# Transformer layer with block-mean attention and 16 experts: block means from turned x on VectorE, another order of projections and spreads, reciprocals and rotations through PSUM, late experts loaded two a pair

## The chip, the cores and the metric

The kernel runs on one core of a Trainium2 chip. The metric is the device time of one execution in microseconds, here the median of three runs.

## The reference

x is 2 batches of 1024 rows of 256. The layer normalises x, adds an attention with 16 heads over 4 key heads, and adds an expert layer in which each row goes to 4 of 16 experts (hidden size 224). The shortened form is:

```python
xn = _layernorm(x, axis=-1)
q_sem, k_sem = split(xn @ Wq_sem, H, DS), split(xn @ Wk_sem, HKV, DS)
q_geo, k_geo = _rope(split(xn @ Wq_geo, H, DG)), _rope(split(xn @ Wk_geo, HKV, DG))
v = split(xn @ Wv, HKV, DV)
# keys and values older than the last 128 positions: one mean per 64 of them
k_sem2, k_geo2, v2 = pool(k_sem), pool(k_geo), pool(v)
scores = (q_sem k_sem2 + q_geo k_geo2) / sqrt(32) * exp(logit_scale)     # masked by position
attn = softmax(scores) @ v2 @ Wo
w, idx = top_k(softmax(xn @ router_w.T + expert_bias), 4)
ffn = sum over the 4 experts of w * (silu(xn @ gate) * (xn @ up)) @ down
return x + attn + ffn
```

Only the last 128 positions keep keys of their own. Before them stand 14 block means of 64 positions, so each query sees at most 142 keys.

## The kernel before

The five engines run programs written out by hand, which wait for one another by semaphores. Rows are handled in 16 tiles of 128: 8 positions ("t") times 2 batches ("u" or "b"). The order of the work is the order in which each engine's function is written. It has five stages.

1. **Head** (0 to about 40 us). Rows are normalised, turned by TensorE into `xT`, projected to keys (k_geo) and router logits. VectorE picks the four experts of each row and computes the place (`slot`) of each row in a list that is sorted by expert. From there on GpSimd scatters the rows into DRAM (`xn_by_expert`, L716): 16 groups of 4 indirect DMAs, and after each group it waits until all 4 have landed. It has nothing else in its queue until then except, in the last four groups, the four halves of the low parts of experts 4 and 5 (`split_low`, L689 to L696). After the groups stand the low parts of experts 6 to 12, and only behind these the scatters of the expert loop (L743).
2. **Keys** (about 40 to 67 us). Block means of x are made by TensorE (`mean_rows`), copied to SBUF, turned back by TensorE and copied again to `x_keys`. Block means of k_geo are made by `block_means`. `rep_keys` makes the keys of each key head; `rope_q` on VectorE (L1148 to L1160) rotates the queries of the last position's tile: bank times cosine to q1, bank times sine to q2, q1 + q2. `bound_tasks` plans which tile of sorted rows belongs to which expert.
3. **Last tile's units** (about 67 to 126 us). The last 128 positions of each batch see all 142 keys. Eight units (2 batches by 4 key heads) go through `l_score` (TensorE), `l_largest` (VectorE), `l_exp` (ScalarE), `l_probabilities` (VectorE), `l_turn` (TensorE), `l_keep` (ScalarE), `l_value` (TensorE) and `l_values` (VectorE). Two score buffers alternate. Beside unit n each engine does a piece of other work (`beside`): folding value means with Wo, tables of the tasks, high and low parts of the first experts' weights.
4. **Pairs** (about 126 to 204 us). The other seven positions see only block means. For each pair of tiles t = 0 to 6: `rope` (VectorE) and `q_turn`, `q_project`, `score`, `p_turn`, `attend` (TensorE), `shifted`, `row_sum`, `probabilities`, `attended` (VectorE), exponentials and copies on ScalarE. `probabilities` (L1297 to L1305) takes one reciprocal of 32 sums into `srec` in SBUF and multiplies `pr` by it in place. SyncE loads the weights of experts 4 to 13 in this stage (`load_late`); ScalarE makes their high parts as `SPLITS` says, in the pair whose number is the place in the list.
5. **Expert loop** (204 to 414 us). 79 tasks of 128 sorted rows. SyncE loads the rows (`xg`) once all scatters of stage 1 have landed (L643 and the wait for `xs_in`), TensorE turns them and multiplies them with high and low parts (L1366 is the line of all its matmuls), ScalarE copies the result to one of four buffers `y` (L939), GpSimd adds it into the output (L743). From the fifth task on the copy waits for the scatter four tasks back, since the buffers are four. Experts 14 and 15 are loaded once the loop has begun.

In the names of the profile `bank` is a PSUM bank, `q` are q1 and q2, `pr` the probabilities of the pairs, `lex` those of the last tile's units, `wgu` and `wdn` expert weights with `_hi` and `_lo` parts, `x_keys` the block means of x and the last 128 positions, `xr` the residual rows.

## Time and profile before

| | us |
|---|---|
| median of 3 runs | 414.18 (413.63 to 416.24) |
| the profiled execution's own time | 415.77 |
| its span, from the first to the last instruction | 414.0 |
| TensorE busy, VectorE, ScalarE, GpSimd | 357.0, 251.3, 184.1, 232.3 |

Busy time of TensorE is modelled from pipelined matmuls. GpSimd's includes its DMA instructions. PEclk in the views is the clock that TensorE was granted, as a share of 2.4 GHz.

### The profile page before, as it was taken

What the parts mean: (1) busy time and instruction counts of PE and PEld (TensorE: products, weight loads), DVE (VectorE), ACT (ScalarE), POOL (GpSimd) and SP (SyncE); (2) the same over time, 40 slices, a digit from 0 to 9 for tenths busy, and PEclk for the clock granted to TensorE, in tenths of its full rate; (3) what the DMA queues carried; (4) which work ended last, traced back from release to release, by engine and by line L of the source; (5) the groups of instructions that cost most, each with busy time, mean ns of one, the idle gap of its engine ahead of it and who ended that gap; (6) DMA issues with size and microseconds to landing.
All of it is one profiled execution on the core that took longest, in us unless ns stands there. A gap on an engine that the chain in (4) does not pass through costs nothing.

```text
span 414.0 us, 8237 instructions
## 1 busy us (share of the span) xinstructions
PE 357.0 (86%) x2103; PEld 287.1 (69%) x2104; DVE 251.3 (61%) x762; ACT 184.1 (44%) x533; POOL 232.3 (56%) x207
## 2 busy tenths in 40 slices
PE   0598997865998999829899799999999999999991
PEld 0493465432665677615688699999999999999881
DVE  3889665446546868897644755555555555555540
ACT  1541345534601445301556545555555555555550
POOL 0600564646653555794076546666666666666664
PEclk9999999889899989986989989999999999999996
DMA  8991121222427996330239647677667767677544
GB/s 255 357 312 37 65 87 55 84 89 81 123 78 226 294 269 194 104 117 13 61 104 247 119 70 114 112 105 112 112 105 110 117 105 110 112 109 110 79 52 51
DMA packets 50095, 52.33 MB, mean 126 GB/s; under 512 B 5633, under 2 KB 47121, under 8 KB 50073
## 3 DMA queue, kind: packets, MB, share of 16 engines
q0 software_dynamic: 14640, 19.34, 28.4%
q1 hardware_dynamic: 35432, 32.73, 28.0%
q8 instruction: 10, 0.16, 0.2%
q14 instruction: 13, 0.10, 0.1%
HBM read 30.14 MB, written 21.91 MB: 126 GB/s over the span
## 4 chain that ended last, share of the span: by engine, by line
PE 72%; DVE 12%; issue 5%; DMA 4%; SPq 3%; ACT 3%; POOLq 1%; DVEq 0%
PE bank L1366 60%; PE bank L1722 4%; PE bank L1746 4%; DMA xg<-xn_by_expert 2%; DMA x_all<-in_L_attn_x 1%; PE bank L1493 1%; PE bank L1526 1%; DVE wgu_lo L1200 1%; DVE lex L1190 1%; ACT x_all L765 1%; DMA out_rows<-y,idx 1%; SPq L636 1%; DVE q L1160 1%; DVE q L1153 1%; DVE q L1156 1%
## 5 line engine op out<-in xcount | busy, mean ns | idle before, releaser
L743 POOL DMA_INDIRECT out_rows<-y,idx x79 | 124.1, 1571 | 71.2 <-ACT y L939 42.1
L716 POOL DMA_INDIRECT xn_by_expert<-x_all,slot_i x64 | 65.2, 1019 | 56.1 <-DMA xn_by_expert<-x_all,slot_i 32.3
L1346 DVE SCALAR_TENSOR_TENSOR act<-bank,xg,sg 128x224 f32<-128x224 f32 x79 | 35.6, 450 | 55.8 <-ACT sg L926 55.8
L1366 PE MATMUL bank<-wgu_hi,xh 128*128 x158 | 65.3, 413 | 2.6 <-DVE wdn_lo L1201 2.5
L1366 PE MATMUL bank<-wgu_lo,xh 128*128 x158 | 58.9, 373 | 0.0
L1366 PE MATMUL bank<-wgu_hi,xl 128*128 x158 | 58.3, 369 | 0.0
L926 ACT ACTIVATE sg<-bank 128x224 f32<-128x224 f32 x79 | 28.3, 359 | 62.5 <-PE bank L1366 62.5
L1366 PE MATMUL bank<-wdn_hi,ah 112*128 x158 | 51.6, 327 | 0.6 <-issue 0.5
L1338 DVE TENSOR_TENSOR xl<-bank,xh 128x256 fp32r<-128x256 f32 x79 | 33.5, 424 | 29.1 <-ACT xh L917 29.1
L1366 PE MATMUL bank<-wdn_hi,al 112*128 x158 | 44.7, 283 | 0.0
L1366 PE MATMUL bank<-wdn_lo,ah 112*128 x158 | 44.5, 281 | 0.0
L939 ACT COPY y<-bank 128x256 f32<-128x256 f32 x79 | 29.5, 374 | 27.7 <-PE bank L1366 27.7
L1366 PEld LDWEIGHTS bank<-wgu_hi,xh 128*128 128x128 f32 x158 | 30.0, 190 | 5.1 <-issue 3.1
L1354 DVE TENSOR_TENSOR al<-bank,ah 112x256 fp32r<-112x256 f32 x79 | 32.7, 414 | 0.5 <-ACT ah L930 0.5
L1722 PE MATMUL bank<-const_k,xg 128*128 128x128 f32 x158 | 30.7, 275 | 2.5 <-DMA xg<-xn_by_expert 2.5
L1366 PE MATMUL bank<-wqg,xT 128*128 128x512 f32 x64 | 32.5, 635 | 0.0
L1366 PEld LDWEIGHTS bank<-wgu_hi,xl 128*128 128x128 f32 x158 | 30.1, 190 | 2.7
L917 ACT CAST xh<-bank 128x256 fp32r<-128x256 f32 x79 | 29.9, 378 | 3.4 <-PE bank L1722 3.0
L1366 PEld LDWEIGHTS bank<-wgu_lo,xh 128*128 128x128 f32 x158 | 30.3, 192 | 1.2
L1366 PEld LDWEIGHTS bank<-wdn_hi,ah 112*128 112x128 f32 x158 | 30.1, 191 | 1.2 <-issue 1.1
L1746 PE MATMUL bank<-const_k,act 128*112 128x128 f32 x158 | 30.3, 273 | 0.0
L1366 PEld LDWEIGHTS bank<-wdn_lo,ah 112*128 112x128 f32 x158 | 30.3, 192 | 0.0
(240 smaller groups left out, 679.4 us busy)
## 6 DMA issues: line engine op xcount, KB each, us to landing
xg<-xn_by_expert SPq DMA_DIRECT2D x79, 129.0 KB, 2.5
wgu<-in_L_ffn_gate_proj SPq DMA_DIRECT2D x16, 224.0 KB, 6.0
wgu<-in_L_ffn_up_proj SPq DMA_DIRECT2D x16, 224.0 KB, 6.7
wdn<-in_L_ffn_down_proj SPq DMA_DIRECT2D x16, 224.0 KB, 7.4
x_all<-in_L_attn_x SPq DMA_DIRECT2D x8, 256.0 KB, 4.6
xr<-in_L_attn_x SPq DMA_DIRECT2D x14, 128.0 KB, 3.3
out_rows<-xr SPq DMA_DIRECT2D x14, 128.0 KB, 1.7
out_rows<-y,idx POOLq DMA_INDIRECT x79, 3.8
```

What stands on the lines that cost most here:

```text
L636: tile = sp.value_load(td_i[0:1, ds(j, 1)], min_val=0, max_val=N * K // P - 1)
L716: gp.indirect_dma_start(xs_d, bass.IndirectOffsetOnAxis(slot_i[:, z, r:r + 1], 0), x_all[:, z, :], None).then_inc(xs_in[p], DMA)
L743: gp.indirect_dma_start(out_rows, bass.IndirectOffsetOnAxis(idx[r % RING][:, 0:1], 0), ysb[r % 4][:, :], None, compute_op=ALU.add).then_in ...
L917: nc.scalar.copy(xh[t.par][:, :, :], bank[t.par][:, 0:D].rearrange("p (c n) -> p c n", c=DC)).then_inc(xh_ready, 1)
L926: nc.scalar.activation(sg[t.par][:, :], bank[2 + t.par][:, 0:I], ACT.Silu).then_inc(sg_ready, 1)
L939: nc.scalar.copy(ysb[t.place][:, :], bank[6 + t.par][:, 0:D]).then_inc(y_ready, 1)
L1338: nc.vector.tensor_tensor(xl[t.par][:, :, :], bank[t.par][:, 0:D].rearrange("p (c n) -> p c n", c=DC), xh[t.par][:, :, :].bitcast(F32), AL ...
L1346: nc.vector.scalar_tensor_tensor(av[t.par][:, :], bank[2 + t.par][:, I:2 * I], xg[t.slot][:, D + 1:D + 2], sg[t.par][:, :], ALU.mult, ALU. ...
L1354: nc.vector.tensor_tensor(al[t.par][:, :, :], bank[4 + t.par][0:IH, 0:2 * P].rearrange("p (c n) -> p c n", c=2), ah[t.par][:, :, :].bitcas ...
L1366: return nc.tensor.matmul(o, lhsT, rhs, start=start, stop=stop)
L1722: last = nc.tensor.transpose(bank[t.par][:, c * P:(c + 1) * P], xg[t.slot][:, c * P:(c + 1) * P], ident)
L1746: last = nc.tensor.transpose(bank[4 + t.par][0:IH, c * P:(c + 1) * P], av[t.par][:, c * IH:(c + 1) * IH], ident)
```

## The change

- **Block means of x.** `mean_rows`, the copy to `x_mean` and the four turns back go. VectorE reduces each `xT[t]` over blocks of 64 columns instead, 14 reductions of 128x256, and scales the 56 means once. ScalarE copies the last position's columns into `x_keys` right after the turns.
- **Order of the keys stage.** TensorE projects the last tile's queries before the rest of the key means, and uses other banks. VectorE rotates the last tile's queries before `weights(1)`; `bound_tasks` moves from ahead of the units to beside unit 1, the spread of its table from unit 1 to 2. The first score no longer waits for `vloc_kept` and `starts_read`. The last two folds stand beside units 3 and 4.
- **Order within the units.** VectorE computes the probabilities of unit n + 1 ahead of the maximum of unit n + 2 and of the side work of unit n. Its low parts of experts 0 and 1 stand beside units 4 and 5.
- **PSUM.** `rope_q` writes bank times cosine back into the bank and adds q2 to that. `srec` becomes two reciprocals of 16 sums each in the bank of the turned probabilities.
- **Late experts.** SyncE loads 4 and 5 ahead of the pairs as before, but 6 to 11 two at a time after the stores of pairs 0, 1 and 2. `SPLITS` moves their high parts one or two pairs later.

```diff
-        RANK_BANK, MEAN_BANK, BLOCK_BANK = 6, 7, 6
-        REP_BANKS = (2, 3, 4, 5, 2, 3, 4, 5)
-        L_Q, L_QS, VLOC_BANK = (7, 0), (1, 2), 6
+        RANK_BANK, BLOCK_BANK = 6, 7
+        REP_BANKS = (4, 5, 0, 1, 4, 5, 7, 0)
+        L_Q, L_QS, VLOC_BANK = (2, 3), (0, 1), 6
         V_BANK, ASEM_BANKS = 4, (0, 4)
-        SPREAD_AT, ASEM_AT = 1, 5
-        FOLDS = {1: (0,), 2: (1,), 3: (2, 3)}
-        FOLD_BANKS = (4, 4, 4, 0)
-        STARTS_BANK = 1
+        SPREAD_AT, ASEM_AT = 2, 5
+        FOLDS = {1: (0,), 2: (1,), 3: (2,), 4: (3,)}
+        FOLD_BANKS = (4, 4, 4, 4)
+        STARTS_BANK = 0
         HIGH_AT = {0: 0, 1: 1, 5: 2}
-        SPLITS = ((), (4, 5), (6, 7), (8, 9), (10,), (), ())
+        SPLITS = ((), (4, 5), (), (6, 7), (8, 9), (10,), ())
         HEAD = (11, 12)
         SENT = 11
         BETWEEN = (4, 5)
...
+            load_residual(1)
             load_late(0)
-            load_residual(1)
-            load_late(1)
-            load_late(2)
-            load_late(3)
             load_residual(REMOTE - 1)
...
             for i in range(REMOTE - 3):
                 store_sum(i)
                 load_residual(i + 2)
-                if i == 1:
+                if i < 3:
+                    load_late(i + 1)
+                else:
                     load_behind(4, 2)
+            store_sum(REMOTE - 3)
             load_behind(5, 4)
-            store_sum(REMOTE - 3)
...
+            act.wait_ge(xT_ready, TB)
+            for b in range(NB):
+                last = nc.scalar.copy(x_keys[:, :, b, NBLK:NKEY], xT[REMOTE][:, b, :, :])
+            last.then_inc(means_kept, 1)
...
-            act.wait_ge(means_done, 1)
-            nc.scalar.copy(x_mean[:, :, :].rearrange("p b n -> p (b n)"), bank[MEAN_BANK][0:NBLK, :]).then_inc(means_rows, 1)
-            act.wait_ge(means_turned, 1)
-            for b in range(NB):
-                at = b * DC * NBLK
-                nc.scalar.copy(x_keys[:, :, b, 0:NBLK], bank[MEAN_BANK][:, at:at + DC * NBLK].rearrange("p (c n) -> p c n", c=DC))
-                last = nc.scalar.copy(x_keys[:, :, b, NBLK:NKEY], xT[REMOTE][:, b, :, :])
-            last.then_inc(means_kept, 1)
...
-            act.wait_ge(hscale_ready, 1)
-            for n in range(HKV):
-                keep_rep(n)
             act.wait_ge(pooled, REMOTE)
             nc.scalar.copy(k_mean[:, :, :].rearrange("p b n -> p (b n)"), bank[BLOCK_BANK][0:NBLK, 0:NB * KD]).then_inc(blocks_rows, 1)
+            for u in range(NB):
+                act.wait_ge(l_qs, u + 1)
+                nc.scalar.copy(qsT[u][:, :, :], bank[L_QS[u]][:, :].rearrange("p (g n) -> p g n", g=HKV)).then_inc(l_qsT, 1)
             act.wait_ge(keys_turned, 1)
             for b in range(NB):
                 nc.scalar.copy(kgeo_t[:, b, 0:NBLK], bank[BLOCK_BANK][:, b * NBLK:(b + 1) * NBLK])
                 last = nc.scalar.copy(kgeo_t[:, b, NBLK:NKEY], bank[BLOCK_BANK][:, (1 + b) * P:(2 + b) * P])
             last.then_inc(keys_kept, 1)
-            act.wait_ge(l_qs, 1)
-            nc.scalar.copy(qsT[0][:, :, :], bank[L_QS[0]][:, :].rearrange("p (g n) -> p g n", g=HKV)).then_inc(l_qsT, 1)
-            for n in range(HKV, 2 * HKV):
+            act.wait_ge(hscale_ready, 1)
+            for n in range(2):
+                keep_rep(n)
+            for u in range(NB):
+                act.wait_ge(l_qt, u + 1)
+                nc.scalar.copy(qrT[u][:, :, :], bank[L_Q[u]][:, :].rearrange("p (g n) -> p g n", g=HKV)).then_inc(l_qT, 1)
+            for n in range(2, 2 * HKV):
...
+
+            def rope_q(raw_bank, u, t, done):
+
+                raw = raw_bank[:, :].rearrange("p (g h d) -> p g h d", g=H, h=2)
+                t2 = q2[:, :].rearrange("p (g h d) -> p g h d", g=H, h=2)
+                co = cos[:, ds(t * RH, RH)].rearrange("p (o d) -> p o d", o=1).to_broadcast([P, 2 * H, RH])
+                for half in range(2):
+                    sn = sin[:, ds(t * DS + half * RH, RH)].rearrange("p (o d) -> p o d", o=1).to_broadcast([P, H, RH])
+                    last = nc.vector.tensor_tensor(t2[:, :, half, :], raw[:, :, 1 - half, :], sn, ALU.mult)
+                link(last)
+                by_half = raw_bank[:, :].rearrange("p (g d) -> p g d", d=RH)
+                link(nc.vector.tensor_tensor(by_half, by_half, co, ALU.mult))
+                nc.vector.tensor_tensor(q1[u][:, :], raw_bank[:, :], q2[:, :], ALU.add).then_inc(done, 1)
+
+            for t in range(REMOTE):
+                dve.wait_ge(xT_ready, t + 1)
+                for b in range(NB):
+                    last = nc.vector.tensor_reduce(x_keys[:, :, b, 2 * t:2 * t + 2], xT[t][:, b, :, :].rearrange("p c (k n) -> p c k n", n=MB), axis=AX.X, op=ALU.add)
+            link(last)
+            nc.vector.tensor_scalar(x_keys[:, :, :, 0:NBLK], x_keys[:, :, :, 0:NBLK], 1.0 / MB, None, ALU.mult).then_inc(means_kept, 1)
+            for u in range(NB):
+                dve.wait_ge(l_q, u + 1)
+                if u:
+                    dve.wait_ge(l_rope, u)
+                rope_q(bank[L_Q[u]], u, REMOTE, l_rope)
...
-                nc.vector.tensor_tensor(q1[u][:, :].rearrange("p (g d) -> p g d", d=RH), raw_bank[:, :].rearrange("p (g d) -> p g d", d=RH), co, ALU.mult)
-                for half in range(2):
-                    sn = sin[:, ds(t * DS + half * RH, RH)].rearrange("p (o d) -> p o d", o=1).to_broadcast([P, H, RH])
-                    last = nc.vector.tensor_tensor(t2[:, :, half, :], raw[:, :, 1 - half, :], sn, ALU.mult)
-                return last
-
-            def rope_sum(u, done):
-                nc.vector.tensor_tensor(q1[u][:, :], q1[u][:, :], q2[:, :], ALU.add).then_inc(done, 1)
...
-                link(rope_q(bank[L_Q[u]], u, REMOTE))
-                rope_sum(u, l_rope)
-            bound_tasks()
...
+                elif n == SPREAD_AT - 1:
+                    bound_tasks()
                 elif n == SPREAD_AT + 1:
                     keep_tables()
-                elif n in (3, 4):
-                    split_low(n - 3)
+                elif n in (4, 5):
+                    split_low(n - 4)
...
             l_largest(0)
             l_largest(1)
+            l_probabilities(0)
             for n in range(UNITS):
-                l_probabilities(n)
+                if n + 1 < UNITS:
+                    l_probabilities(n + 1)
                 if n + 2 < UNITS:
                     l_largest(n + 2)
...
-                link(rope_q(bank[2 + u], u, t.number))
-                rope_sum(u, c_rope[u])
+                rope_q(bank[2 + u], u, t.number, c_rope[u])
...
-                nc.vector.reciprocal(srec[:, :, :], ssum[:, :, :]).then_inc(c_rec, 1)
+                srec = [turned_bank(u, t)[:, 0:H] for u in range(NB)]
+                for u in range(NB):
+                    last = nc.vector.reciprocal(srec[u], ssum[:, u, :])
+                last.then_inc(c_rec, 1)
                 dve.wait_ge(c_rec, t.count(1))
                 for u in range(NB):
-                    nc.vector.tensor_tensor(by_key(pr[u], t), by_key(pr[u], t), over_heads(srec[:, u, :], t), ALU.mult).then_inc(c_p[u], 1)
+                    nc.vector.tensor_tensor(by_key(pr[u], t), by_key(pr[u], t), over_heads(srec[u], t), ALU.mult).then_inc(c_p[u], 1)
...
-            def mean_rows(t):
-
-                return mm(bank[MEAN_BANK][0:NBLK, :], sums_of(t), x_all[:, NB * t:NB * (t + 1), 0:D], t == 0, t == REMOTE - 1)
-
...
-            for t in range(4):
-                mean_rows(t)
+            block_means(0)
+            block_means(1)
             pe.wait_ge(chosen_ready, 1)
...
-            for t in range(4, REMOTE):
-                last = mean_rows(t)
-            last.then_inc(means_done, 1)
-            pe.wait_ge(means_rows, 1)
-            for b in range(NB):
-                for c in range(DC):
-                    at = (b * DC + c) * NBLK
-                    last = nc.tensor.transpose(bank[MEAN_BANK][:, at:at + NBLK], x_mean[:, b, c * P:(c + 1) * P], ident[0:NBLK, 0:NBLK])
-            last.then_inc(means_turned, 1)
+            block_means(2)
+            block_means(3)
...
-            pe.wait_ge(slots_ready, 1)
-            block_means(0)
-            block_means(1)
-            pe.wait_ge(kv_in, 4 * DMA)
-            pe.wait_ge(wrep_ready, DC * (G + 2))
-            pe.wait_ge(means_kept, 1)
-            for n in range(HKV):
-                rep_keys(n)
-                block_means(2 + n)
-            block_means(REMOTE - 1)
+            pe.wait_ge(q_in, 2 * DMA)
+            for u in range(NB):
+                for c in range(DC):
+                    last = mm(bank[L_Q[u]][:, :], xT[REMOTE][:, u, c, :], wqg[:, c, :], c == 0, c == DC - 1)
+                last.then_inc(l_q, 1)
+            for t in range(4, REMOTE):
+                block_means(t)
             pe.wait_ge(rope_done, TB)
+            for u in range(NB):
+                for g in range(HKV):
+                    for c in range(DC):
+                        last = mm(bank[L_QS[u]][:, g * P:(g + 1) * P], wqs[:, c, g * P:(g + 1) * P], xT[REMOTE][:, u, c, :], c == 0, c == DC - 1)
+                last.then_inc(l_qs, 1)
...
+            pe.wait_ge(kv_in, 4 * DMA)
+            pe.wait_ge(wrep_ready, DC * (G + 2))
+            pe.wait_ge(means_kept, 2)
+            for n in range(2):
+                rep_keys(n)
             for u in range(NB):
-                for c in range(DC):
-                    last = mm(bank[L_Q[u]][:, :], xT[REMOTE][:, u, c, :], wqg[:, c, :], c == 0, c == DC - 1)
-                last.then_inc(l_q, 1)
-            l_sem(0)
+                pe.wait_ge(l_rope, u + 1)
+                turn_queries(bank[L_Q[u]], u).then_inc(l_qt, 1)
+            pe.wait_ge(l_qsT, NB)
+            for n in range(2, HKV):
+                rep_keys(n)
...
-            pe.wait_ge(starts_ready, 1)
-            pe.wait_ge(l_qsT, 1)
-            mm(bank[STARTS_BANK][:, 0:NT * E], ones[0:1, :], at_of(left[:, :, :])[0:1, 0:NT * E], True, True).then_inc(starts_spread, 1)
-            pe.wait_ge(rep_kept, HKV + 1)
-            l_sem(1)
...
-                    pe.wait_ge(vloc_kept, 1)
                     pe.wait_ge(masks_ready, 3)
-                    pe.wait_ge(starts_read, 1)
...
                 if n == 0:
                     rep_values()
+                    pe.wait_ge(starts_ready, 1)
+                    mm(bank[STARTS_BANK][:, 0:NT * E], ones[0:1, :], at_of(left[:, :, :])[0:1, 0:NT * E], True, True).then_inc(starts_spread, 1)
...
```

VectorE's order in the units, before (units 1 and 2; `lex` and `lrec` alternate between two buffers, `lneg` is the negated maximum, `oT` the attended values):

```order
L1187 RECIPROCAL lrec_211<-lsum_209 128x4
L1188 TENSOR_TENSOR pr_64<-lex_205,lrec_211 128x4x14
L1190 TENSOR_TENSOR lex_205<-lex_205,lrec_211 128x4x128
L1180 TENSOR_REDUCE lneg_207<-bank 128x2 x2
L1196 COPY oT_213<-bank 128x256
L1187 RECIPROCAL lrec_210<-lsum_208 128x4
L1188 TENSOR_TENSOR pr_64<-lex_204,lrec_210 128x4x14
L1190 TENSOR_TENSOR lex_204<-lex_204,lrec_210 128x4x128
```

And after, from the first unit on:

```order
L1181 RECIPROCAL lrec_208<-lsum_206 128x4
L1182 TENSOR_TENSOR pr_64<-lex_200,lrec_208 128x4x14
L1184 TENSOR_TENSOR lex_200<-lex_200,lrec_208 128x4x128
L1181 RECIPROCAL lrec_209<-lsum_207 128x4
L1182 TENSOR_TENSOR pr_64<-lex_201,lrec_209 128x4x14
L1184 TENSOR_TENSOR lex_201<-lex_201,lrec_209 128x4x128
L1174 TENSOR_REDUCE lneg_204<-bank 128x2 x2
L1159 TENSOR_TENSOR vb<-bank,const_c 128x4x56
```

The probabilities of the second unit now stand ahead of the first side work instead of behind it, and so on through all units.

SyncE's queue in the pairs, after: the load of experts 6 and 7 (`wgu`, `wdn`) behind the store of pair 0 (`out_rows`) and the residual rows of pair 2 (`xr`):

```order
L588 DMA out_rows<-xr_0_72 128x256
L588 DMA out_rows<-xr_0_74 128x256
L583 DMA xr_0_72<-in_L_attn_x 128x256
L583 DMA xr_0_74<-in_L_attn_x 128x256
L400 DMA wgu<-in_L_ffn_gate_proj 128x2x224
L401 DMA wgu<-in_L_ffn_up_proj 128x2x224
L402 DMA wdn<-in_L_ffn_down_proj 112x2x256
L400 DMA wgu<-in_L_ffn_gate_proj 128x2x224
L401 DMA wgu<-in_L_ffn_up_proj 128x2x224
L402 DMA wdn<-in_L_ffn_down_proj 112x2x256
```

Before, all 24 loads of experts 4 to 11 stood ahead of the first of these stores.

## Rows read from the trace of the kernel before

**Rows 1.** Stages: busy time of each engine, granted clock, DMA share, GB/s.

```profile
40.36:62.00 21.64, 21.10 (x92) 12.16 (x89) 14.97 (x47) 8.64 (x23) 12.79 (x16) 1.00 0.20 71
67.34:111.81 44.47, 31.99 (x172) 18.13 (x171) 22.76 (x65) 23.36 (x83) 26.17 (x30) 0.88 0.26 88
111.81:126.20 14.39, 13.79 (x60) 9.73 (x59) 8.02 (x16) 2.75 (x8) 7.71 (x10) 1.00 0.24 84
204.40:224.49 20.09, 19.40 (x112) 17.30 (x112) 10.40 (x33) 11.32 (x33) 12.61 (x8) 0.92 0.63 167
224.49:236.00 11.51, 8.10 (x51) 7.05 (x52) 9.21 (x21) 8.23 (x20) 7.21 (x5) 1.00 0.77 145
236.00:405.20 169.20, 168.62 (x1113) 156.49 (x1114) 91.18 (x275) 88.56 (x276) 107.20 (x70) 0.99 0.66 102
```

**Rows 2.** The same view of pairs 0, 4, 5 and 6.

```profile
126.20:134.60 8.40, 7.06 (x40) 4.93 (x41) 5.43 (x14) 1.40 (x3) 3.80 (x5) 1.00 0.90 265
...
163.60:172.00 8.40, 8.40 (x49) 6.28 (x48) 7.30 (x20) 3.40 (x8) 6.55 (x7) 1.00 0.50 173
172.00:196.00 24.00, 14.02 (x56) 8.49 (x54) 21.94 (x24) 2.85 (x9) 18.26 (x12) 0.79 0.19 56
196.00:204.40 8.40, 7.35 (x48) 5.79 (x47) 5.12 (x14) 3.98 (x10) 0.00 (x0) 1.00 0.16 49
```

**Rows 3.** Chain that ended last, in the units: start, us, engine, tile, line.

```profile
68.19 1.56 ACT lex L836 x8
...
94.19 1.00 DVE wgu_lo L1200
...
96.04 0.70 DVE lex L1190
...
96.78 0.66 PE bank L1526 x4
97.44 1.42 PE bank L1366 x10
...
98.89 0.81 DVE lneg L1180 x2
```

**Rows 4.** Timeline at pair 5: start, us, engine, line, operation, tiles.

```profile
174.08 2.09 POOL L693 TENSOR_TENSOR wgu_lo<-wgu,wgu_hi  x1 [0.74 <-DMA xn_by_expert<-x_all,slot_i]
174.17 0.32 DVE L1291 TENSOR_TENSOR pr<-bank,smax 128x160 f32<-128x160 f32 x1
176.25 11.15 DVE L1305 TENSOR_TENSOR pr<-pr,srec 128x160 f32<-128x160 f32 x2
187.19 2.16 POOL L693 TENSOR_TENSOR wgu_lo<-wgu,wgu_hi  x1
```

**Rows 5.** All rotations' sums, L1160: ns min/median/max.

```profile
L1160 DVE TENSOR_TENSOR q<-q,q x16: 691/692/2494, 56.3 to 193.0; 128x512 f32<-128x512 f32 x16
```

**Rows 6.** Scatter of rows: DMA from issue to landing, 40 to 126 us, then 126 to 175.

```profile
DMA to landing us min/median/max: 2.4/2.6/4.5
...
DMA to landing us min/median/max: 2.4/4.6/8.1
```

**Rows 7.** GpSimd's timeline: first and twelfth group, then the loop's first scatter.

```profile
41.30 1.03 POOL L716 DMA_INDIRECT xn_by_expert<-x_all,slot_i  x1 [0.59 <-POOL x_all L706]
...
125.91 0.97 POOL L716 DMA_INDIRECT xn_by_expert<-x_all,slot_i  x1 [2.66 <-DMA xn_by_expert<-x_all,slot_i]
...
216.25 1.62 POOL L743 DMA_INDIRECT out_rows<-y,idx  x1 [1.10 <-ACT y L939]
```

**Rows 8.** ScalarE's timeline: the copy of the fifth task's result.

```profile
224.49 0.37 ACT L939 COPY y<-bank 128x256 f32<-128x256 f32 x1 [0.30 <-PE bank L1366]
```

**Rows 9.** DMA issues: KB each, us to landing.

```profile
xg<-xn_by_expert SPq DMA_DIRECT2D x79, 129.0 KB, 2.5
...
out_rows<-y,idx POOLq DMA_INDIRECT x79, 3.8
```

**Rows 10.** VectorE's timeline in the head: one reduction of 128x256.

```profile
32.68 0.42 DVE L1041 TENSOR_REDUCE weight_sum<-weight_dense 128x16 f32<-128x256 f32 x1
```

More of the change, by code:

```diff
@@ L178, in build @@
         smax = [wat.take(f"smax{u}", [P, H]) for u in range(NB)]
-        ssum, srec = (wat.take(n, [P, NB, H]) for n in ("ssum", "srec"))
+        ssum = wat.take("ssum", [P, NB, H])
         wl = r_loop[0]
@@ L233, in build @@
         kgeo_t = wa.take("kgeo_t", [P, NB, NKEY])
-        x_mean = wa.take("x_mean", [NBLK, NB, D])
         k_mean = wa.take("k_mean", [NBLK, NB, KD])
@@ L292, in build @@
         wl = Region(l_at, S_SIZE - (l_at - s_at))
+        lex = [wl.take(f"lex{q}", [P, G, NKEY]) for q in range(2)]
         qsT = [wl.take(f"qsT{u}", [P, HKV, P]) for u in range(NB)]
-        lex = [wl.take(f"lex{q}", [P, G, NKEY]) for q in range(2)]
         lneg = [wl.take(f"lneg{q}", [P, G]) for q in range(2)]
@@ L1524, in l_turn @@
                     pe.wait_ge(l_pT, n)
+                else:
+                    pe.wait_ge(vloc_kept, 1)
                 for h in range(G):
```

38 lines of the change are left out of this document (8 added, 30 removed).

## The prediction

> **What bounds the kernel now.** I read the table of stages first. In the expert loop from 236 us TensorE is busy 168.6 of 169.2 us at the full clock [rows 1]: that stage is TensorE's own work and the change leaves it alone, so only its start can move. Before it TensorE is idle 12.5 of 44.5 us in the last tile's units, where its clock falls to 0.88 on average [rows 1]. A pair takes 8.4 us with TensorE busy throughout (pair 4), but pair 5 takes 24.0 with TensorE busy 14.0 [rows 2]. Then I read the chain of waits in the units [rows 3], the timeline at pair 5 [rows 4], and last GpSimd's own chain, which is off the path today: scatters from 41.3 us [rows 7] to 174 [rows 4], then seven pairs of low parts, then the first scatter of the loop at 216.25. Since the change shortens the stages beside it, I ask of each stage what it leaves for this chain.
>
> **Keys stage: last tile's units begin 5 us earlier.** From 40.36, where the first weights are done, VectorE is busy 14.97 us up to 62.00 and otherwise waits [rows 1], mostly for TensorE. The plan of tasks after 62.00 moves behind the first unit. New are 14 reductions of 256 elements. One alone takes 0.42 [rows 10]; back to back I take 0.35, so 4.9, and 0.2 for the scale. Each rotation gets one more link, some 0.1 us. So VectorE's work is 15.0 + 5.1 + 0.2 = 20.3, and with 1 us of gaps between linked instructions it ends at 61.6. TensorE's chain in the new order (block means as the rotations of k arrive, projections, keys) comes to its first score at about 60.7 and ends it near 62.2. The first maximum, which stood just inside the 67.34 boundary, then starts at 62.3: -5.0. The means' old way (copies and turns) cost nothing on the path by itself; its bound from below is 0, from above these 5 us. The two waits that leave the first score (table read, local values) are inside the same figure.
>
> **Units: 11 us less.** Today's chain goes, for one unit: probabilities, turn 0.66, score 1.42, maximum 0.81, copy of values, side work (a low part: 1.0 and more), and only then the next probabilities (the link at 96.04 takes 0.70) [rows 3]. The next unit's exponentials have long been ready. With its probabilities computed first, what ties unit n to n + 2 is probabilities 1.0, turn 0.66, score 1.42, maximum 0.81, exponentials 1.56 [rows 3] and waits, 5.7 us for two units. That is below the engines' own sums, so these decide. I walked the eight units through the three queues with these durations and the side work where it now stands: probabilities end at 65.7, 67.3, 72.0, 77.6, 81.2, 86.3, 90.3 and 94.4, and the projection with Wo that began at 111.81 begins at 95.7. The check on this: TensorE's work in the stage is 32 us at a clock of 0.88 [rows 1], some 29 at full clock, and 95.7 - 62.3 = 33.4. So -16.1 at that place, 5.0 of it from the keys. What follows up to 126.20 has TensorE busy 13.8 of 14.4 [rows 1] and keeps its length: the pairs begin at 110.1. The value means travel through DRAM meanwhile; their fold comes later by one unit, and I count 8 us of slack for them.
>
> **Pairs.** At 176.25 VectorE starts two products `pr` times `srec` that take 11.15 us, while GpSimd runs low parts back to back (174.08 to 187.19 and on) [rows 4]. In the same moments the difference of a bank and `smax`, at 174.17, takes 0.32 at the same width [rows 4], so two such would take 0.64 and the excess is 10.5. The held ones have two SBUF inputs. So has the sum of a rotation: 16 of them, 0.692 in the median, 2.494 at most [rows 5]. After the change both have one input in PSUM. The Trainium skill ("SBUF — State Buffer", "Who interferes with whom") says that a VectorE instruction with two SBUF inputs and a GpSimd instruction that reads SBUF exclude each other, and that the second blocks until the first finishes. That the form with PSUM passes, the trace agrees with. That a hold ends with one GpSimd instruction it contradicts: those take 2.1, so two holds would come to 4.2 at most and the rest of the 10.5 would have another cause and stay; by the rows all of it goes.
> I take pairs 0 and 4 at their 8.4 and 1, 2, 3 at 8.5, so 42.3; pair 5 at 10.3 (8.4 and 1.9 for two chunks of probabilities); pair 6 at 8.4 up to the first turned rows of the loop [rows 2]. By this the loop could start at 110.1 + 42.3 + 10.3 + 8.4 = 171.1. Two small costs: the link and the second reciprocal, 0.1 to 0.2 each time, lie under TensorE, which never waits in pair 4; bound 0 to 3 us. And the late experts. Their load now follows the store of the pair before; 6 DMAs of 224 KB at the 265 GB/s of pair 0 [rows 2] take 5.1 us, and ScalarE asks for them 10 to 11 us after that store. I expect it to wait 1 us in each of pairs 3, 4 and 5: +3, bound 0 to 9. So 174.1, against 204.4.
>
> **What is late next: GpSimd.** The scatters land at 174.05 today: GpSimd waits for the last one and starts low parts at 174.08 [rows 4]. Eleven groups take 125.91 - 41.30 = 84.6, 7.69 each [rows 7]. Undisturbed, 16 would end at 41.3 + 15 x 7.69 + 7.0 = 163.7; beside the loads of experts landing grows from 2.6 to 4.6, 8.1 at most [rows 6]. The change brings the same bytes in smaller portions over more groups. I leave the end at 174.05 (bounds 163.7 and, all seven groups from 110 us at 8.1 us, 163.7 + 7 x 5.5 = 202.2). The loop's rows are loaded behind it, 2.5 from issue to landing [rows 9] and 0.8 for SyncE's and TensorE's steps: first turn at 177.4.
> Then GpSimd does seven experts' low parts ahead of its first scatter. Four took 187.19 - 174.08 = 13.1 [rows 4], so 3.28 each and 23.0 in all: 197.0, and 1.1 as today ahead of the scatter: 198.1 [rows 7]. It lands 3.8 later [rows 9]. Only then may ScalarE write the fifth task's result, at 202.0; by TensorE it would be ready at 177.4 + 20.1 = 197.5. Today that copy is at 224.49 [rows 8]. From there everything follows as before: -22.5. What the wait adds by a lower clock (rows 1 show 0.92 over the loop's first 20 us) I set against what it hides of TensorE's idle 3.4 us between 224.5 and 236 [rows 1]: 0.
>
> **Sum.** Span 414.0 - 22.5 = 391.5. The profiled execution took 415.77, 1.59 above the median of 414.18, so by its own time 393.3 and by the median 391.7. Of 5 + 11 + 13 us gained ahead, 8 go to a chain that was hidden. Without GpSimd's chain the sum would be 204.4 - 174.1 = 30.3, so 384.
>
> **Rivals.**
> A. *The pairs stay the bound, since the units gain little.* For it: three queues that wait on one another rarely keep a hand-made schedule, and TensorE's clock falls when it idles. Against it: the chain's side work is plain in the rows. With no gain in the units the loop starts at 174.1 + 11 = 185.1 and nothing behind it waits: 185.1 + 209.6 = 394.7, by the median 394.9. 0.20.
> B. *Smaller portions disturb the scatters less.* They land at 166: low parts end at 189.0, first scatter lands at 193.9; the loop starts by the pairs at 174.1, its fifth result at 194.2: -30.3, 384. For it: a portion ends before the group's last DMA in about half the cases. 0.20.
> C. *They disturb more groups.* With landing doubled in seven groups, 163.7 + 7 x 2.6 = 181.9, 7.8 later: 399.5. The Trainium skill ("DMA: Bandwidth & Descriptors", the paragraph on arbitration) has each DMA engine take turns between its queues packet by packet, which is this case for as long as a load lasts. The rows (2.6 and 4.6) are near it. 0.12.
> D. *Slower than before.* The same mechanism at its worst: each group waits the full 8.1. The scatters land at 202.2, 28.2 later: 391.7 + 28.2 = 419.9. It decides from a mean landing of 7.3 us in the seven groups on, (196.6 - 163.7) / 7 + 2.6. Against it: today's median under a heavier load is 4.6. 0.03.
> E. *The PSUM operand does not end the hold.* The back-to-back low parts fall behind the pairs now, so only the four inline halves hold the pairs, by up to 1 us each. The loop would start at 178.1, still under GpSimd's bound: 391.7 too. The trace would tell, not the time; it is part of the forecast.
>
> **How the numbers follow.** Forecast 0.43 (387 to 396), A 0.20, B 0.20, C 0.12, D 0.03, and 0.02 that some new wait takes nearly all. The range reaches from below B to above C: 382 to 401. A measurement of this kernel tells about 1% from no change. Faster by more: 0.95. Within: 0.02. Slower: 0.03.
>
> **What would show it.** Right: the first maximum near 62, no unit longer than 6 us, the pairs' start near 110; both L1305's and L1160's successors without any instance over 1 us; scatters landed near 174; low parts of experts 6 to 12 without a gap of 17 us among them, the loop's first scatter near 198 and ScalarE's fifth copy waiting for it. Wrong: pair 5 still above 15 us; ScalarE waiting for expert loads over 3 us in a pair; scatters landed after 182 or before 168; the loop from its fifth task on slower than 2.35 us a task.

## The result and the profile after

Four executions of the changed kernel took 394.55 us in the median (390.10 to 399.95), four of the kernel before beside them 415.21. The ratio is 0.947, with an interval of 0.938 to 0.956; ratios leave out executions more than 1.5% above the fastest of their kernel, here the one of 399.95 us. The profiled execution of the changed kernel took 395.17 us with a span of 393.4; the forecast was 391.7 us and a span of 391.5. A second measurement gave 395.13 us and 0.950 (0.944 to 0.957).

The stages of the kernel after, cut at the same places as [rows 1] (busy time of each engine, granted clock, DMA share, GB/s):

```profile
60.97:96.94 35.97, 32.36 (x174) 19.00 (x172) 24.92 (x78) 22.75 (x83) 20.90 (x22) 0.86 0.25 82
96.94:111.36 14.42, 13.79 (x61) 9.75 (x59) 8.15 (x16) 2.76 (x8) 9.08 (x10) 1.00 0.29 103
178.72:203.34 24.62, 23.17 (x127) 20.50 (x128) 9.96 (x30) 11.62 (x34) 23.85 (x16) 0.86 0.58 149
203.34:214.90 11.56, 7.10 (x37) 6.09 (x35) 8.48 (x19) 8.29 (x20) 9.68 (x6) 0.85 0.78 114
214.90:384.60 169.70, 168.85 (x1113) 156.62 (x1114) 91.58 (x277) 88.55 (x276) 107.53 (x70) 0.99 0.65 102
```

The units last 36.0 us instead of 44.5, what follows them 14.4 as before, and the long loop 169.7 instead of 169.2: it has only moved. The third line is the loop's beginning up to the fifth result; there GpSimd is busy 23.85 of 24.62 us, where it was busy 12.61 of 20.09.

The seven pairs in the same view:

```profile
111.36:121.66 10.30, 8.85 (x41) 5.64 (x41) 5.66 (x14) 1.40 (x3) 4.09 (x5) 0.83 0.73 223
121.66:132.14 10.48, 9.90 (x55) 6.62 (x55) 8.35 (x26) 4.82 (x11) 6.04 (x7) 1.00 0.33 102
132.14:140.50 8.36, 8.36 (x50) 6.02 (x48) 6.11 (x17) 1.78 (x5) 4.20 (x6) 1.00 0.67 205
140.50:148.78 8.28, 8.28 (x50) 6.19 (x49) 6.93 (x20) 4.68 (x10) 5.72 (x6) 1.00 0.77 241
148.78:157.22 8.44, 8.44 (x49) 6.30 (x48) 7.51 (x22) 4.30 (x10) 3.76 (x5) 1.00 0.81 257
157.22:168.21 10.99, 10.61 (x55) 7.09 (x53) 9.07 (x25) 4.36 (x12) 7.59 (x8) 1.00 0.83 252
168.21:175.54 7.33, 7.33 (x47) 5.75 (x46) 4.15 (x12) 3.58 (x9) 3.75 (x4) 1.00 0.77 243
```

Pair 5, the sixth line, takes 11.0 us; it took 24.0 [rows 2]. No instruction with the new operand is long. The products with the reciprocals and the sums of the rotations (ns min/median/max), against 11.15 us for two products [rows 4] and 2.494 us for the longest sum [rows 5]:

```profile
L1305 DVE TENSOR_TENSOR pr<-pr,bank x14: 180/284/389, 124.6 to 177.2; 128x32 f32<-128x32 f32 x2, 128x64 f32<-128x64 f32 x2, 128x96 f32<-128x96 f32 x2, 128x128 f32<-128x128 f32 x2
L1084 DVE TENSOR_TENSOR q<-bank,q x16: 691/691/692, 49.4 to 165.3; 128x512 f32<-128x512 f32 x16
```

What ends last now. GpSimd's timeline: its first and last low part behind the scatters, and the loop's first scatter:

```profile
175.91 2.07 POOL L691 TENSOR_TENSOR wgu_lo<-wgu,wgu_hi  x1 [3.33 <-DMA xn_by_expert<-x_all,slot_i]
177.95 1.25 POOL L694 TENSOR_TENSOR wdn_lo<-wdn,wdn_hi  x1
...
195.68 2.12 POOL L691 TENSOR_TENSOR wgu_lo<-wgu,wgu_hi  x1
197.76 1.28 POOL L694 TENSOR_TENSOR wdn_lo<-wdn,wdn_hi  x1
199.20 1.62 POOL L741 DMA_INDIRECT out_rows<-y,idx  x1 [0.16 <-issue]
```

and ScalarE's copies of the fourth and fifth results:

```profile
198.93 0.38 ACT L930 COPY y<-bank 128x256 f32<-128x256 f32 x1 [0.31 <-PE bank L1366]
203.34 0.37 ACT L930 COPY y<-bank 128x256 f32<-128x256 f32 x1 [2.33 <-DMA out_rows<-y,idx]
```

The fourth copy was released by TensorE, the fifth by the first scatter's landing. At 2.38 us a task it would have stood at 201.3. So the chain that was hidden before holds the fifth result by 2.0 us. It also sets the loop's beginning: TensorE is idle 3.2 us ahead of 178.72, until the first rows have come in behind the scatters. The chain that ended last in this trace names it, with 14% for the DMA of the scatters of rows and 13% for their issue, where the page of before had TensorE with 72% and none of these scatters.

### The profile page after: what moved, and what is told of

The parts are those of the page before. It is cut to its first block, busy times and chain, and to the rows that moved or that the text cites. A ratio compares the mean times of both kernels' runs of the same rounds, so it can differ in the third digit from the quotient of the medians.

```text
span 393.4 us, 8217 instructions
## 1 busy us (share of the span) xinstructions
PE 350.6 (89%) x2085; PEld 287.6 (73%) x2086; DVE 242.4 (62%) x784; ACT 182.6 (46%) x530; POOL 232.0 (59%) x207
## 4 chain that ended last, share of the span: by engine, by line
PE 48%; DMA 18%; POOL 14%; issue 9%; DVE 6%; ACT 2%; POOLq 1%; SPq 1%; DVEq 0%; ACTq 0%
PE bank L1366 39%; DMA xn_by_expert<-x_all,slot_i 14%; POOL xn_by_expert L714 13%; PE bank L1728 4%; PE bank L1704 4%; DMA out_rows<-y,idx 2%; DMA x_all<-in_L_attn_x 1%; ACT x_all L763 1%; POOL wgu_lo L691 1%; DVE stats L954 1%; PE bank L1378 1%; DVE logit_left L1024 1%; DMA xg<-xn_by_expert 1%; POOLq L103 0%; ACT wgu_hi L815 0%
## 5 line engine op out<-in xcount | busy, mean ns | idle before, releaser
L714 POOL DMA_INDIRECT xn_by_expert<-x_all,slot_i x64 | 66.2, 1034 | 55.6 <-DMA xn_by_expert<-x_all,slot_i 33.7
```

The lines of the kernel that those rows point to most:

```text
L714: gp.indirect_dma_start(xs_d, bass.IndirectOffsetOnAxis(slot_i[:, z, r:r + 1], 0), x_all[:, z, :], None).then_inc(xs_in[p], DMA)
```

## The experiments

Ratios are to the kernel before, measured beside each kernel. Beside the first four runs (units' order alone, PSUM operands alone, SBUF again, low parts left out) the kernel before took 407.5 to 416.0 us, elsewhere 408.6 to 417.6 with most above 413; their ratios therefore may read up to 1% high, and I compare these four by their times. The times of before go with TensorE's clock: of its 35 executions in this section the 5 with a mean granted clock of 0.96 or more took 409.7 us on average, the 16 below 0.95 took 415.0. A size from these four runs is therefore uncertain by 3 to 4 us, and what they show rests on their traces.

**One part alone, and one part undone.** Before, with the units' order alone:

```diff
+            l_probabilities(0)
             for n in range(UNITS):
-                l_probabilities(n)
+                if n + 1 < UNITS:
+                    l_probabilities(n + 1)
```

> The kernel before, with one edit: each unit's probabilities are computed one unit ahead, as in the changed kernel. Rotations and reciprocals keep their SBUF operands, the late experts load as before. Theory 1 (the hold by GpSimd's back-to-back low parts catches whichever pair's products fall into it): the units end 11 us earlier, pairs start near 115; GpSimd begins its low parts at 174 as before, and now pair 6's products fall into them instead of pair 5's and are held some 10 us; the loop starts 11 us earlier, span near 403, time near 404. Theory 2 (the hold is a matter of pair 5 alone, and once the pairs are early enough it is gone): loop starts 21 us earlier, then GpSimd's chain sets the end: span near 392, time near 393. Theory 3 (the units gain little): pairs start after 122, time above 410.

Measured: 399.97 us, ratio 0.976 (0.967 to 0.985), against a median of 412.5 for before: 12.5 less, by the ratio only 2.4% or some 10. The profiled execution took 408.4, 8 above the rest, with a mean granted clock of 0.945 where the rest had 0.961 to 0.966, so its rows show where time goes and the median shows how much. VectorE's timeline:

```profile
165.02 2.44 DVE L1307 TENSOR_TENSOR pr<-pr,srec 128x160 f32<-128x160 f32 x2
174.91 12.11 DVE L1307 TENSOR_TENSOR pr<-pr,srec 128x192 f32<-128x192 f32 x2
```

Before, the long hold was on the products with 160 columns, which stand beside TensorE's pair 5. Now these take 2.44 us, and the long hold is on the next ones, with 192 columns beside pair 6, since these are what GpSimd's low parts (from 174.87 on) now meet: theory 1, for the place. For the size the median is 4 us below what theory 1 gave; whether the hold is shorter in the other executions no trace shows. Theory 3 falls: the pairs start at 118.9.

Before, with the PSUM operands alone:

```diff
-                nc.vector.tensor_tensor(q1[u][:, :], q1[u][:, :], q2[:, :], ALU.add).then_inc(done, 1)
+                nc.vector.tensor_tensor(q1[u][:, :], raw_bank[:, :], q2[:, :], ALU.add).then_inc(done, 1)
...
-                nc.vector.reciprocal(srec[:, :, :], ssum[:, :, :]).then_inc(c_rec, 1)
+                srec = [turned_bank(u, t)[:, 0:H] for u in range(NB)]
```

> The kernel before, with one edit: the sum of each rotation and the product with the reciprocals take one operand from PSUM. Theory 1 (an operand in PSUM passes GpSimd): no instruction of the two groups above 1 us, pair 5 takes 10 to 13 us instead of 24, the loop starts near 192 and TensorE, not GpSimd, sets the fifth result: span near 402, time near 403. Theory 2 (the port is held for either form): products of 10 us again, time 415 as before.

Measured: 403.3 us, ratio 0.986 (0.975 to 0.997): 9.2 less than the median of before, by the ratio only 1.4% or some 6. All its products:

```profile
L1305 DVE TENSOR_TENSOR pr<-pr,bank x14: 181/284/389, 139.7 to 191.7; 128x32 f32<-128x32 f32 x2, 128x64 f32<-128x64 f32 x2, 128x96 f32<-128x96 f32 x2, 128x128 f32<-128x128 f32 x2
```

Theory 1: pair 5 takes 10.4 us (172.3 to 182.7), with GpSimd's low parts running from 173.5 to 189.9 beside its products.

The changed kernel with the two SBUF forms again (the diff above, turned round):

> The changed kernel with the two SBUF forms of before put back (rotation sum, product with the reciprocals). Theory 1: GpSimd's back-to-back low parts begin at 175.9 and the last pair's products, which end at 177.5, fall into them: held some 8 to 10 us, so the loop's first gate products and with them the fifth result come 5 to 8 us later: time 399 to 403. Theory 2 (the pairs now finish ahead of the low parts, so the form no longer matters): time as the changed kernel, near 394.5, with at most two held instructions of 2 us.

Measured: 400.45 us, ratio 0.980 (0.968 to 0.992), 5.3 to 5.9 us above the changed kernel, and 4.9 in the spans. The last pair's products, and TensorE's turn that waits for them:

```profile
180.16 8.52 DVE L1301 TENSOR_TENSOR pr<-pr,srec 128x224 f32<-128x224 f32 x2
```

```profile
187.36 0.69 PE L1603 MATMUL bank<-const_k,pr 128*128 128x128 f32 x2 [6.04 <-DVE pr L1301]
```

Theory 1. So the operand matters in the changed kernel too, in its last pair, which the prediction had thought to be ahead of the low parts.

The changed kernel with the units' old order (the first diff, turned round):

> The changed kernel with one edit undone: a unit's probabilities are computed only after the side work of the unit before. Theory 1 (the order of the units is worth 11 us, and it reaches the end once the pairs are the bound): pairs start near 122, the loop near 189, the fifth result comes from TensorE near 212 and no longer waits for GpSimd: 7 to 9 us longer than the changed kernel. Theory 2 (scatters and GpSimd's low parts hide most of it): 0 to 3 us longer.

Measured: 404.88 us, ratio 0.975 (0.968 to 0.982), 9.8 us above the changed kernel on the same chip. Pairs start at 127.7, and the fifth result is copied at 214.75 without a wait for a scatter. Theory 1, and a little more than its 7 to 9. The clock has a part in that size: the units took 53.0 us here at 0.74, where before, with the same order of probabilities, they took 44.5 at 0.88.

The changed kernel with the late loads where they were:

```diff
-            load_residual(1)
             load_late(0)
+            load_residual(1)
+            load_late(1)
+            load_late(2)
+            load_late(3)
...
-        SPLITS = ((), (4, 5), (), (6, 7), (8, 9), (10,), ())
+        SPLITS = ((), (4, 5), (6, 7), (8, 9), (10,), (), ())
```

> The changed kernel with one edit undone: experts 4 to 11 are again loaded in one go ahead of the pairs, 12 in pair 1, 13 behind pair 5, and their high parts stand where they stood before. Theory 1 (where the loads stand matters little; the smaller portions cost ScalarE its 12 to 15 us of waits for experts, of which at most 4 reach TensorE, and in return the burst of 5.4 MB against the scatters is gone): ScalarE's waits for expert loads under 5 us in sum, scatters landed between 172 and 180, time within 3 us of the changed kernel's 394.9. Theory 2 (the smaller portions disturb the scatters more, as rival C says): scatters landed before 172, time 4 us shorter or more. Theory 3 (the burst disturbs them more): scatters landed after 181, time 4 us longer or more.

Measured: 392.95 us, ratio 0.953 (0.945 to 0.960): no difference that can be told from the changed kernel's 0.947 and 0.950. Scatters landed at 173.1 and ScalarE waited for no expert, against 10.4 us in the changed kernel (15.4 in its second trace). Theory 1. In this trace the loop began at 176.1, 2.6 us sooner than in the changed kernel's first one, and GpSimd's low parts 2.8 us sooner. The fifth copy came 2.7 us sooner, at the end of a longer wait for the first scatter:

```profile
200.66 0.37 ACT L931 COPY y<-bank 128x256 f32<-128x256 f32 x1 [3.63 <-DMA out_rows<-y,idx]
```

**Both of the first two parts, and nothing else.**

> The kernel before with both edits together: probabilities one unit ahead, and the PSUM operands. What is still missing of the change is the new keys stage (which in the changed kernel starts the units 6 us earlier), the new places of the side work and the late loads two a pair. Pairs start near 119 (as with the first edit alone) and the loop some 64 us later (as with the second alone), near 183; GpSimd's scatters land near 174 and its fifth-result bound stands near 202, TensorE's near 204. Theory 1 (once the pairs are early enough GpSimd's chain sets the end, so that the missing 6 to 9 us are mostly hidden): 393 to 397, at most 2 us above the changed kernel. Theory 2 (the pairs' start decides to the end): 400 to 403.

Measured: 394.8 us, ratio 0.954 (0.949 to 0.959), beside 0.947 and 0.950 for the whole change. For the time theory 1: two edits give the whole gain within what can be measured. Alone they took 12.5 and 9.2 us off by the medians (2.4 and 1.4% by the ratios), together 19.4 (4.6%), so the times leave open whether anything is missing to the sum. The trace shows a part that is hidden: its fifth copy waits 4.6 us for GpSimd:

```profile
196.46 0.37 ACT L939 COPY y<-bank 128x256 f32<-128x256 f32 x1 [0.31 <-PE bank L1368]
203.15 0.37 ACT L939 COPY y<-bank 128x256 f32<-128x256 f32 x1 [4.63 <-DMA out_rows<-y,idx]
```

This trace shows more than it was made for. The new keys stage is missing, its first maximum stands at 66.44, not 60.97, and yet the pairs start at 111.08, not 111.36. TensorE's clock tells most of why. The changed kernel, then this one, then the units' order alone, in slices of 4 us (the third number from the end is the granted clock):

```profile
60.00:64.00 4.00, 2.43 (x18) 1.19 (x14) 2.90 (x9) 2.18 (x12) 2.10 (x3) 1.00 0.27 99
64.00:68.00 4.00, 3.51 (x20) 2.47 (x20) 2.25 (x6) 3.06 (x10) 2.80 (x3) 0.76 0.18 66
68.00:72.00 4.00, 4.00 (x17) 3.29 (x17) 1.51 (x7) 1.32 (x8) 1.51 (x4) 0.50 0.18 66
72.00:76.00 4.00, 4.00 (x17) 2.19 (x16) 1.02 (x3) 1.94 (x3) 3.15 (x3) 0.50 0.19 68
76.00:80.00 4.00, 4.00 (x23) 1.95 (x21) 3.54 (x18) 2.61 (x10) 1.29 (x3) 0.96 0.18 66
```

```profile
68.00:72.00 4.00, 2.04 (x15) 1.33 (x15) 2.76 (x8) 3.69 (x17) 1.62 (x2) 1.00 0.18 66
72.00:76.00 4.00, 4.00 (x36) 3.22 (x35) 2.83 (x10) 3.68 (x13) 2.47 (x4) 1.00 0.28 101
```

```profile
68.00:72.00 4.00, 1.94 (x16) 1.20 (x14) 2.73 (x8) 3.69 (x18) 1.38 (x4) 1.00 0.18 66
72.00:76.00 4.00, 4.00 (x20) 3.21 (x16) 0.89 (x3) 2.82 (x10) 3.08 (x4) 0.51 0.19 68
76.00:80.00 4.00, 4.00 (x18) 2.71 (x17) 1.86 (x7) 1.94 (x3) 1.70 (x3) 0.50 0.18 66
```

Between the second scores and the first turned probabilities TensorE idles 2.06 us in all three. In the changed kernel the granted clock is then at its lower level (0.50, 1.2 GHz) for 10 us, with TensorE busy throughout. In the second kernel the same pause left the clock at 1.00, and the third, with the same order of work there, fell. So the 6.4 us that the keys stage gained were lost again in the units: 36.0 us at 0.86 against 29.7 at 1.00. Not all of this is the clock: 10 us at half of it are 5 us of work by an estimate, and the changed kernel also has `bound_tasks` and other side work in other places there.

The Trainium skill ("TensorE: Matmul & The Clock Gate", "Part 1: The HAM clock gate") says that the chip looks at TensorE in windows that run free of the program, so that one kernel changes level at different moments in different runs. The second and third trace, alike in this place and yet apart, agree with that. A single trace doesn't price this pause, then: the changed kernel's units ran at 0.86 and 0.87 in its two traces, at 0.86 with the loads put back, and at 0.95 in the last trace of the version below. But chance alone doesn't fit all executions. The mean granted clock over the whole span was 0.970 to 0.977 in all six executions of the kernel with two edits, and 0.949 to 0.970 in all eight of the changed kernel. The kernel before had 0.942 to 0.962 beside it, no more than elsewhere, so it is hardly the chip. Something in the order of the work seems to favour the first; what it is was not tried.

The clock also limits what this run says about theory 1. Its fifth result was ready near 198.8 (196.46 and one task of 2.38) and held until 203.15, so 4.3 us were hidden. Had the pairs begun near 119, as expected, the copy would by this estimate have come some 3.6 us later, near 206.8, and the time would have lain between the two theories.

**Is GpSimd's chain the bound, and what is behind it?** The changed kernel with less for GpSimd to do. The low parts of experts 9 to 12 are left out (zeros stand in for them):

```diff
-            with gp.Fori(BETWEEN[-1] + 1, IN_LOOP) as e:
+            with gp.Fori(BETWEEN[-1] + 1, 9) as e:
...
+            for e in range(9, IN_LOOP):
+                nc.gpsimd.memset(of_expert(wgu_l, e).bitcast(F32), 0.0)
+                nc.gpsimd.memset(of_expert(wdn_l, e).bitcast(F32), 0.0).then_inc(w_lo, 1)
```

> The changed kernel, with the low parts of experts 9 to 12 left out on GpSimd (eight fills with zeros in their place, by an estimate from the 0.31 us fill of 128x256 some 1.3 us an expert instead of 3.3); the rest is the same work. Theory 1 (GpSimd's low parts ahead of the loop's first scatter set the fifth result): first scatter near 191, the fifth result leaves TensorE's bank near 201.3 instead of 203.3, gaps of 2.2 and 0.9 us and the low clock behind them are gone: span 3 to 5 us shorter, time near 390. Theory 2 (scatters and pairs, which both end at 175.5, set the end, and GpSimd's low parts have slack): time as the changed kernel, near 394.5.

Measured: 392.24 us (391.49 to 392.34), span 390.4, 3.0 less in the traces and 2.3 to 2.9 in the medians. The first scatter is issued at 192.3, the fifth copy stands at 200.57 and waits for no scatter. Theory 1, at the lower end of its range; 2.4 us of waiting for expert 15's low part stayed, as in the changed kernel (2.6). By the ratio, 0.957 (0.948 to 0.966), no gain over the changed kernel can be told, so the trace carries this and the time only agrees with it.

The changed kernel again, for the comparison with the next two:

> The changed kernel as it is, to stand beside the next three on one chip. The first measurement gave 0.947 of the kernel before and a span of 393.4 us: expected again, with the scatters landed near 175.5 and the fifth result copied near 203.

Measured: 395.13 us, ratio 0.950 (0.944 to 0.957), span 393.3. Inside the span things stood otherwise: ScalarE waited up to 7.0 us for an expert, TensorE 4.3 us in pairs for that, the scatters landed at 178.5, the loop began at 184.2 instead of 178.7, and the fifth copy waited only 1.0 us for the first scatter. The chain that ended last doesn't run through the scatters of rows here. It runs from the store of a pair's sums to a late expert's load behind it, which ScalarE waits for, and on through TensorE and the pairs (start, us, engine, what):

```profile
150.53 7.38 DMA out_rows<-xr
162.38 5.84 DMA wdn<-in_L_ffn_down_proj
168.24 0.94 ACT wgu_hi L815
170.06 3.62 PE bank L1366 x8
```

So the two bounds lie within a few microseconds of each other, and in this execution the pairs set the loop's beginning. Of the 5.5 us by which it began later, 3.9 are TensorE's waits for late experts (4.3 against 0.4), and about 2 come from the units (38.1 us instead of 36.0).

The low parts of experts 6 and 7 by VectorE, all computed (`MIDDLE` is (6, 7), `MIDDLE_AT` is (4, 5)):

```diff
                 probabilities(t)
+                if t.number in MIDDLE_AT:
+                    e = MIDDLE[MIDDLE_AT.index(t.number)]
+                    dve.wait_ge(w_hi, e + 1)
+                    nc.vector.tensor_tensor(of_expert(wgu_l, e), of_expert(wgu, e), of_expert(wgu_h, e).bitcast(F32), ALU.subtract)
+                    nc.vector.tensor_tensor(of_expert(wdn_l, e), of_expert(wdn, e), of_expert(wdn_h, e).bitcast(F32), ALU.subtract).then_inc(w_mid, 1)
...
```

> The changed kernel, with the low parts of experts 6 and 7 computed by VectorE at the ends of pairs 4 and 5 (1.8 us each) instead of by GpSimd (3.3 each); all is computed. Theory 1 (GpSimd's chain sets the fifth result): first scatter of the loop 6.6 us earlier, near 192.6, the fifth result at TensorE's pace near 201, span 2 to 4 us shorter than the changed kernel's. Theory 2 (pairs set the end and have no room on VectorE): each low part lengthens its pair by up to 1.8 us, so the span is 0 to 3 us longer.

Measured: 391.73 us, ratio 0.942 (0.936 to 0.947), 3.4 us below the changed kernel in the medians, though the intervals overlap a little. The first scatter came at 193.9, near theory 1's 192.6; in this trace the loop began 3.1 us later than in the changed kernel's first one, so the fifth copy stood at 203.5 again, but it waited for no scatter. Theory 1, for the scatter and for the median; its fifth result near 201 didn't come.

With experts 13 to 15 one task earlier besides:

```diff
-                if j.counts is None and j.r in (5, 6, 7):
-                    split_late(IN_LOOP + j.r - 5)
+                if j.counts is None and j.r in (4, 5, 6):
+                    split_late(IN_LOOP + j.r - 4)
...
-                if j.counts is None and j.r in (6, 7, 8):
+                if j.counts is None and j.r in (5, 6, 7):
...
```

> The kernel of the run before, and besides the high and low parts of experts 13 to 15 one task earlier in the loop (ScalarE behind tasks 4 to 6, VectorE 5 to 7). Theory 1 (the 2.5 us that TensorE waits at the loop's ninth task for expert 15's low part is the next bound, and starting it one task earlier removes it): another 2 to 2.5 us less, span near 388. Theory 2 (ScalarE and VectorE have no room for these parts in any task, so the delay only moves): span as the run before, within 1 us. Theory 3 (the load of experts 14 and 15, issued near 192, lands after 201 and ScalarE now waits for it): 0 to 3 us longer.

Measured: 389.69 us, ratio 0.938 (0.928 to 0.948), span 385.5. The wait for expert 15 is gone from TensorE's list: theory 1 for the wait. The gain of 2.0 us in the medians lies within the intervals. Once more in five rounds:

> The version with the low parts shared and experts 13 to 15 one task earlier, once more and in more rounds, for its interval: ratio to the kernel before 0.938 expected, that of the changed kernel being 0.947 to 0.950.

Measured: 389.70 us, ratio 0.944 (0.938 to 0.950), span 386.6. That is 5 us below the changed kernel in the medians, though the intervals of the ratios overlap.

And with the late loads as before the change:

> The version with the low parts shared and experts 13 to 15 one task earlier, and besides the loads as in the run before this one. By theory 1 of that run within 3 us of that version's 389.7 us; by theory 2 about 385; by theory 3 over 393.

Measured: 386.81 us, ratio 0.933 (0.927 to 0.940), the fastest of all: theory 1 by 0.1 us, near theory 2. Its profiled execution took 393.1 and another 393.8, against four of 385.9 to 387.0, so the trace tells only what went wrong in a long one: a scatter group landed late, at 181.5 the low parts began, and TensorE waited 11.9 us for the loop's first rows. In both comparisons (this one, and the changed kernel with its loads put back) the old place of the loads has the lower median, by 2.9 and by 1.6 to 2.2 us: no run shows a gain from loading two a pair.

**One number for all.** The time from the fifth copy to the end of the span, each from its own trace: before 189.5, units' order alone 189.9, PSUM alone 189.7, SBUF again 188.9, units back 188.7, both parts 189.0, loads back 188.8, low parts left out 189.8, low parts shared 188.8, changed 190.1. That is the carrying step of the prediction ("from there everything follows as before"), and it holds over a range of 24 us in the copy's place. Only where the wait for expert 15 is gone is it less: 385.5 - 200.15 = 185.4, 386.6 - 201.57 = 185.0 and, with the old loads, 391.3 - 206.14 = 185.2. The changed kernel's second trace, at 187.3, is the one exception.

## Why the prediction came out as it did

**Right, by its mechanism, in the first trace.** The end follows from the fifth copy, and the fifth copy waits for GpSimd. In the second trace it still does, but only by 1.0 us, and there the pairs set the loop's beginning. The terms of the forecast and what the first trace has for them: scatters landed 174.05 and 175.5 to 175.9; seven low parts 23.0 and 23.1 (175.91 to 199.04); first scatter of the loop 198.1 and 199.2; landing 3.8 and 4.1; fifth copy 202.0 and 203.34; shift from there -22.5 and -21.2; span 391.5 and 393.4. Of the 1.9 us, 1.3 stand at the copy, from the scatters' landing, and 0.6 come behind it, where the clock is 0.85 up to 214.90. The SBUF-SBUF hold and its end by an operand in PSUM are shown from both sides by two kernels (PSUM alone, SBUF again). The Trainium skill's rule ("SBUF — State Buffer", "Who interferes with whom") fits in what it locks, and the traces disagree again with a hold of one instruction: 12.11 and 8.52 us for two products beside GpSimd instructions of 2.1 and 1.3.

**Right in the sum, off in the terms.** The keys stage gave 6.4 us, not 5. The units gave 8.5, not 11: the walk through the queues took TensorE's 29 us at full clock, and it worked 32.4 at 0.86. Both together -14.9 against -16.1, and the pairs begin at 111.4, not 110.1. The trace with the clock at 1.00 took 29.7 us for the units, less than the walk's 33.4, so with the new order and a full clock the forecast gain is there; the clock was the term left out. Pairs 0 to 4 took 45.9 us, not 42.3: pair 0 10.3 instead of 8.4 (clock 0.83), pair 1 10.5 instead of 8.5. In the trace of before the same five take 45.8 us, so nothing had made them shorter; the forecast gave pairs 1 and 2 the length of later pairs. (Its sum also names 13 us for the pairs, where its own terms, 78.2 before and 64.0 after, give 14.2.) In return the late experts cost TensorE 0.4 us, not 3, in the first trace: ScalarE waited 3.5 and 4.7 us, over the 3 that the prediction named as a sign against it, but its queue had that much room. In the second trace they cost 4.3. From their beginning to 175.54, where TensorE's work in them ends, the pairs came to 64.2 us as forecast (64.0). That is luck: the errors cancelled.

**What the prediction missed.** It said that 8 of some 30 us gained ahead go to GpSimd's chain, but not which parts of the change are then worth little. By the run with two edits alone (ratio 0.954 against 0.947 and 0.950), the keys stage, the new places and the late loads together have less than 1% in the end. That isn't only the hidden chain, as the prediction would have it: the clock took back what the keys stage gave. Also wrong was "the back-to-back low parts fall behind the pairs now": they met the last pair (products at 176.9, low parts from 175.9), and with the old operands that costs 5 us.

**The rivals.** A (units gain little, 394.7) names nearly the time measured, nearer than the forecast does, but not the place: the first trace has the loop at 178.7 and the fifth copy waiting for the scatter, A had 185.1 and no wait. The second trace, with the loop at 184.2 and a wait of 1.0, is close to A's place, though not by A's cause: its units took 38.1 us against 44.5, and waits for late experts made the loop late. B and D didn't occur. C needed scatters at 181.9; they landed at 175.5 and 178.5, and at 173.1 with the loads moved back. Since these last differ by 3 us between two executions of one kernel, no effect of the portions on the scatters can be told. E is refuted.

## What to carry to other kernels

When one chain is shortened, put a number on each chain that was hidden beside it, and carry the gain only to the first of them; parts of the change that come after that are worth little until the next chain moves too. A wait of one engine for another's port isn't tied to the place where the trace shows it: it follows whatever instruction meets the other engine's burst, so a kernel in which the work has moved must be searched for it again (putting the old operands back costs 5 us in the changed kernel, in another pair). And a pause of some 2 us in TensorE's work can be followed by a stretch at half the clock that costs nearly as much as was saved ahead of it (some 5 of 6.4 us here).

## What the runs showed that was not expected

- The same pause of 2.06 us ahead of the first unit's turns was followed by the clock at 0.50 for 10 us in one kernel and at 1.00 in another with nearly the same work there: 6.3 us apart in the units (35.97 and 29.66).
- VectorE computes an expert's low parts in 1.8 us, GpSimd in 3.3, and pair 5 with one of them in it grew only from 11.0 to 11.9 us.
- One program's stages differ more between executions than its time does: the loop of the changed kernel began at 178.7 in one trace and at 184.2 in the other, with spans of 393.4 and 393.3. Why the loads of the late experts and the scatters land at such different times was not tried.
